# More output buffers, later sends and a cast on another engine in a fused GCN and mixture-of-experts kernel

## The chip, the cores and the metric

The kernel runs on one core of one Trainium2 chip. The metric is device time in microseconds of one execution, the median of several.

## What is computed

6250 nodes with 256 channels and 106,250 edges, then a layer with 16 experts of which each node uses two:

```python
def _L0_gnn_ref(x, edge_index, W1, b1, W2, b2):     # theta: GCN of the normalised x, averaged over nodes
    theta = _gcn_conv(x, edge_index, W1, b1)
    theta = jax.nn.relu(jnp.mean(theta, axis=0))
    theta = 2.0 * jax.nn.sigmoid(theta @ W2 + b2) - 1.0
    coefs = theta.reshape(C, 2 * k) * lambdas + init_v
    out = x[:, :, None] * coefs[None, :, :k] + coefs[None, :, k:]
    return jnp.max(out, axis=-1)

x = x + _L0_gnn_ref(_layernorm(x, axis=-1), edge_index, ...)
# feed-forward part, on layernorm(x):
topk_vals, topk_idx = jax.lax.top_k(x @ gate_w + gate_b, 2)
h = relu(x @ w1[e] + b1[e]); expert_out = h @ w2[e] + b2[e]      # for the two chosen experts
y = x + sum(softmax(topk_vals) * expert_out)
x = x + layernorm(y) * gamma + beta
```

Because theta is a mean over nodes, the aggregation needs only one weight per node: the degree of every node, its inverse root, and for each edge the value at the target added up at the source.

## The kernel before, in words

The code is written by hand for each engine: each has its own instruction list, in the order in which it runs, and semaphores tie them together. There are five stages.

**Degree stage.** Edges lie on 128 partitions in 832 columns, 26 groups of 32. For each group VectorE makes two one-hot arrays of the target (`onehot`, line 1288, called from the loop at line 1292), and TensorE multiplies them into the degree table (line 1020). Beside it ScalarE takes sums and squares of the 49 node tiles of x (lines 785 and 798). Behind the loop VectorE finishes the variance (line 1304) and ScalarE takes its root (line 817); the inverse root and the shift (lines 1323, 1324) follow, then the root of the degrees (line 819).

**Values stage.** For each group g of 32 edge columns VectorE selects keys (`select`, line 1315), makes two one-hots of the source (line 1288), casts the gathered values from PSUM (line 1351) and weighs the one-hot with them (line 1356, twice). TensorE runs in 104 slots, four to a group. Slot n is `rows_of(n)` (line 1040), `values_of(n - 1)` (line 1051) and `scatter(n - 8)` (line 1060). ScalarE masks each slot's rows (line 832) and puts the 49 normalising passes of x (line 842) between them. Group g's first rows need `select(g)`, and its weighted one-hots need the cast of its 64 value columns.

```python
dve.wait_ge(masked_free, 4 * g + 4)
nc.vector.tensor_copy(g16[:, u], PS[:, B_G + u, 0:2 * GC]...).then_inc(g_copied, 1)
```

**Routing stage.** Affine, maximum, second normalisation, gate, top two and slot numbers in eight groups of node tiles. GpSimd scatters each token row twice into its expert's place in `xs` (98 indirect DMAs, line 575). A tile of expert work needs that its rows have landed: the first ten tiles (`SOON`) need the first six groups, all others need all 98 scatters and 16 pad rows blocks (`pad_row`, one DMA of 128 rows per expert, issued by SyncE and ScalarE).

**Tile stage.** 113 tiles of 128 rows. TensorE runs `up(t)` (line 1224), `turn_x(t + 1)` (line 1212) and `down(t - 1)` (line 1235). VectorE runs in iteration t: `relu` (line 1562), `home_of(t + 1)` (lines 1572 and 1575), `share_of(t + 1)` (lines 1581 to 1585), `weigh_out(t - 1)` (line 1603) and `base_of(t)` (line 1594). GpSimd sends each finished tile from one of `OBUFS` buffers to `ys` by an indirect DMA with the row numbers in `home` (`send`, line 582). `down(t)` waits for `weigh_out(t - 1)`. The row numbers lie in 4 buffers, the outputs in 4; `home_of(t)` from tile 4 on waits until the send of tile t - 4 has landed:

```python
dve.wait_ge(o_sent[(t - XBUFS) % OBUFS], 16 * ((t - XBUFS) // OBUFS + 1))
```

GpSimd's list puts the first four sends between the last group's scatters. SyncE, in iteration t, issues the load of the weights of tile t + 4 and of the rows of tile t + 4; the iteration that loads tile 10 first waits for all scatters and all pads (lines 702 to 705).

**Last stage.** The two expert rows of each node are summed, normalised, scaled and stored, behind the landing of every send.

## Time and profile before

| | us |
|---|---|
| median of 3 runs (928.9 to 932.2) | 929.2 |
| the profiled execution's own time | 929.78 |
| its span, first to last instruction | 928.0 |
| TensorE busy | 770.7 (83%) |
| VectorE busy | 675.1 (73%) |
| ScalarE busy | 460.1 (50%) |
| GpSimd busy | 273.9 (30%) |
| mean granted TensorE clock | 0.911 |

An engine's busy time is summed over stages that have different limits, so the shares do not say what bounds a stage. The views below are read per stage; their times count from the start of the span. A wait is named after the instruction that came last. The granted clock is 1.0 at 2.4 GHz and 0.5 at 1.2 GHz, so a mean of 0.95 is a mix of the two.

### The profile page before, as it was taken

How to read it: one execution, taken by the hardware profiler on the slowest of the kernel's cores; microseconds unless marked ns; L12 is line 12 of the kernel's file. 1: busy time of each engine (PE TensorE's matmuls, PEld its weight loads, DVE VectorE, ACT ScalarE, POOL GpSimd, SP SyncE). 2: the span in 40 equal slices, each digit the busy share in tenths (PEclk: the TensorE clock that was granted, in tenths of full speed). 3: DMA queues.
4: the chain of work that ended last, by engine and by line, in shares of the span. 5: the costliest groups of instructions: out<-in, count | busy, mean ns of one | idle time of the engine just before them, and what ended most of it. 6: DMA issues, size and time to landing. Idle time of an engine off the chain costs nothing.

```text
span 928.0 us, 21948 instructions
## 1 busy us (share of the span) xinstructions
PE 770.7 (83%) x6539; PEld 673.4 (73%) x6539; DVE 675.1 (73%) x1856; ACT 460.1 (50%) x1161; POOL 273.9 (30%) x309
## 2 busy tenths in 40 slices
PE   3554988787866787676999999999999999997882
PEld 3454455555545786565899999999999999996771
DVE  6999899999927677854666666666666666664597
ACT  6980887787726657333333334433344333443253
POOL 9300000000001467777334444444322222222000
PEclk9999699999986667559899999999999999999896
DMA  9831444456155354269766666676766666662984
GB/s 275 233 116 35 129 162 144 143 163 196 59 182 171 100 171 137 104 228 288 207 215 215 214 211 212 210 214 215 213 213 207 211 216 213 212 211 64 380 313 135
DMA packets 88003, 174.88 MB, mean 188 GB/s; under 512 B 13067, under 2 KB 57022, under 8 KB 84796
## 3 DMA queue, kind: packets, MB, share of 16 engines
q1 hardware_dynamic: 74600, 143.83, 49.4%
q0 software_dynamic: 10512, 27.88, 8.5%
q10 hardware_dynamic: 2776, 1.77, 0.9%
q8 instruction: 56, 0.92, 0.4%
q14 instruction: 59, 0.48, 0.2%
HBM read 136.24 MB, written 37.20 MB: 187 GB/s over the span
## 4 chain that ended last, share of the span: by engine, by line
PE 54%; DVE 24%; issue 10%; POOL 7%; DMA 2%; ACT 2%; SPq 0%; DVEq 0%; POOLq 0%; ACTq 0%
PE PS L1224 21%; PE PS L1235 21%; DVE W L1288 10%; POOL xs L575 7%; DVE W L1315 3%; DVE W L1356 3%; PE PS L1212 3%; PE PS L1150 2%; PE PS L1265 2%; DVE W L1657 1%; DVE W L1664 1%; PE PS L1126 1%; DVE W L1634 1%; DMA ys<-W,R 1%; PE PS L1004 1%
## 5 line engine op out<-in xcount | busy, mean ns | idle before, releaser
L1224 PEld LDWEIGHTS PS<-R,W 128*128 128x128 f32 x1808 | 221.2, 193 | 7.6 <-ACT R L926 1.7
L1235 PE MATMUL PS<-W,R 128*128 x904 | 216.1, 382 | 9.9 <-DVE W L1603 8.3
L1224 PE MATMUL PS<-R,W 128*128 128x128 f32 x1808 | 222.0, 276 | 1.0 <-ACT R L926 1.0
L582 POOL DMA_INDIRECT ys<-W,R x113 | 109.8, 972 | 267.2 <-DVE W L1603 261.8
L1235 PEld LDWEIGHTS PS<-W,R 128*128 128x128 f32 x904 | 165.1, 193 | 28.9 <-issue 11.0
L926 ACT ACTIVATE R<-PS 128x256 f32<-128x256 f32 x113 | 43.6, 386 | 264.6 <-PE PS L1212 262.3
L1288 DVE TENSOR_TENSOR W<-R,W 128x3136 bf16<-128x3136 bf16 (+1 forms) x104 | 157.0, 1565 | 0.7 <-PE PS L1020 0.5
L1562 DVE TENSOR_SCALAR R<-PS,b1T 128x128 f32<-128x128 f32 x226 | 69.3, 349 | 113.8 <-PE PS L1224 109.5
L832 ACT ACTIVATE W<-PS 128x1024 f16<-128x1024 f32 x104 | 105.5, 1020 | 34.3 <-PE PS L1040 33.0
L575 POOL DMA_INDIRECT xs<-W,slot_i x98 | 98.0, 1000 | 80.0 <-DVE slot_i L1454 51.3
L1040 PE MATMUL PS<-W,table 114*128 114x512 f16 x208 | 68.4, 414 | 24.1 <-DVE W L1315 23.6
L943 ACT ACTIVATE R<-PS,b1T 128x128 f32<-128x128 f32 x226 | 70.4, 368 | 2.3 <-PE PS L1224 2.1
L1060 PE MATMUL PS<-W 128*98 128x128 bf16 x832 | 69.2, 228 | 2.7 <-DVE W L1356 2.7
L1020 PE MATMUL PS<-W 128*64 128x98 bf16 x832 | 42.7, 208 | 30.8 <-DVE W L1288 30.8
L567 POOL MEMSET R<- 128x261 f32 x1 | 0.3, 318 | 229.7 <-PEq L1082 229.7
L1051 PEld LDWEIGHTS PS<-sel,W 128*128 128x128 f16 x832 | 31.9, 98 | 46.2 <-ACT W L832 38.8
L1020 PEld LDWEIGHTS PS<-W 128*64 128x64 bf16 x832 | 39.3, 110 | 34.1 <-DVE W L1288 34.1
L952 ACT ACTIVATE W<-R 128x256 f32<-128x256 f32 x113 | 57.9, 513 | 4.3 <-DVE R L1572 4.3
L1060 PEld LDWEIGHTS PS<-W 128*98 128x98 f16 x832 | 56.3, 129 | 2.9 <-DVE W L1356 2.9
L1603 DVE SCALAR_TENSOR_TENSOR W<-PS,R,W 128x256 f32<-128x256 f32 x113 | 54.7, 484 | 5.0 <-PE PS L1235 4.8
L1265 PE MATMUL PS<-W,ident 128*128 128x256 f32 x196 | 47.2, 403 | 13.2 <-DMA W<-ys 8.0
L1265 PEld LDWEIGHTS PS<-W,ident 128*128 128x128 f32 x196 | 39.3, 203 | 21.1 <-DMA W<-ys 8.7
(249 smaller groups left out, 1117.0 us busy)
## 6 DMA issues: line engine op xcount, KB each, us to landing
W<-in_L_ffn_w SPq DMA_DIRECT2D x129, 512.0 KB, 3.7
W<-key_rows SPq DMA_DIRECT2D x26, 784.0 KB
R<-xs SPq DMA_DIRECT2D x113, 130.5 KB, 2.6
W<-ys SPq DMA_DIRECT2D x4, 2048.0 KB, 13.7
XH<-in_x SPq DMA_DIRECT2D x6, 896.0 KB, 11.8
out<-W SPq DMA_DIRECT2D x4, 1024.0 KB, 5.1
W<-in_x SPq DMA_DIRECT2D x4, 896.0 KB, 5.8
W<-key_rows SPq DMA_DIRECT2D x52, 64.0 KB
```

The costliest lines, as they stand in the source:

```text
L575: nc.gpsimd.indirect_dma_start(out=xs[:, :], out_offset=bass.IndirectOffsetOnAxis(ap=slot_i[0:rows, g % XNBUFS, j, k:k + 1], axis=0), in_= ...
L582: nc.gpsimd.indirect_dma_start(out=ys[:, :], out_offset=bass.IndirectOffsetOnAxis(ap=home[:, b:b + 1], axis=0), in_=O3[o], in_offset=None) ...
L832: act.activation(masked[0:2 * HD, n % 3, :].rearrange("p (h m) -> p h m", h=2), PS[0:2 * HD, bank:bank + 2, :], ACT.Relu).then_inc(masked_ ...
L943: last = act.activation(HT3[:, u, j, :], PS[:, 2 + 2 * u + j // 2, (j % 2) * P:(j % 2 + 1) * P], ACT.Relu, bias=b1T[:, ds(e, 1), j])
L1020: last = nc.tensor.matmul(PS[0:HD, B_DEG, 0:LOD], oh_hi[g % 2][:, c // 2, :, c % 2], oh_lo[g % 2][:, c // 2, 0:LOD, c % 2], start=(g == 0 ...
L1040: last = nc.tensor.matmul(PS[0:2 * HD, B_R + 2 * (n % 2) + h, :], table[0:KT, :], oh_t[0:KT, g % 2, at:at + 4 * P], start=True, stop=True)
L1060: last = nc.tensor.matmul(PS[0:2 * NT, B_ACC, 0:P], weighted[g % 2][:, c // 2, :, c % 2], oh_lo[g % 2][:, c // 2, :, c % 2], start=(n == 0 ...
L1224: last = nc.tensor.matmul(PS[:, 2 + 2 * u + j // 2, (j % 2) * P:(j % 2 + 1) * P], W1S[b][:, k, j * P:(j + 1) * P], XT3[:, u, k, :], start= ...
L1235: last = nc.tensor.matmul(PS[:, 6, 0:C], HT3[:, u, j, :], wt2(e * W2COLS, j), start=(j == 0), stop=(j == 3))
L1265: last = nc.tensor.matmul(y_sum(g, j), ident[:, :], y_two[g % YBUFS][:, j, k, :], start=(k == 0), stop=(k == 1))
L1288: return nc.vector.tensor_tensor(into, pairs_of.to_broadcast([P, GC // 2, size, 2]), iota2[:, 0:size, :].unsqueeze(1).to_broadcast([P, GC ...
L1562: last = nc.vector.tensor_scalar(HT3[:, u, j, :], PS[:, 2 + 2 * u + j // 2, (j % 2) * P:(j % 2 + 1) * P], b1T[:, ds(e, 1), j], 0.0, ALU.ad ...
```

## The change

It has five parts.

1. `OBUFS` goes from 4 to 8, and `home` gets a ring of its own of `HBUFS` = 12. `home_of(t)` waits for a send only from tile 12 on, `weigh_out(t)` from tile 8 on. The buffers Z1 and Z3 of the tile stage move to the space of gW2 to make room.
2. GpSimd issues all 98 scatters first and every send after them.
3. The 16 pads are spread over six tiles: SyncE issues two ahead of the loop and one in each of six iterations, ScalarE two in each of iterations 0 and 1 and one in each of 2 to 5. The loads of gamma and beta go from iteration 4 to 6.
4. The variance, inverse root and shift are computed inside VectorE's degree loop (behind groups 20 and 21), and ScalarE does 28 of the 49 normalising passes there, ahead of the root of the degrees. The other 21 follow one to a group, behind slots 4k + 3.
5. The cast of the values goes from VectorE to ScalarE. The cast of group g stands behind the masking of slot 4g + 5.

```diff
@@ -65,7 +65,7 @@
 W2COLS = C * F // P
 W1BUFS = 4
 XW = C + 5
-XBUFS, OBUFS = 4, 4
+XBUFS, OBUFS, HBUFS = 4, 8, 12
 SOON, SOON_G = 10, 5
 XNBUFS = 3
 X_AT = E * WCOLS * 4 - 2 * GT * C * 4
@@ -210,12 +210,10 @@
         share = take([XBUFS], fp32)
         first = take([XBUFS], fp32)
         weight = take([XBUFS], fp32)
-        home = take([XBUFS], i32)
+        home = take([HBUFS], i32)
         assert at[0] <= RB
         take, at = carve(W, D_AT + 4 * XNBUFS * GT * XW)
         O3 = [take([C], fp32) for _ in range(OBUFS - 1)] + [O_last]
-        Z1 = take([2, C], fp32)
-        Z3 = take([2, C], fp32)
         assert at[0] <= D_AT + 4 * (XNBUFS * GT * XW + GT * 2 * P)
 
         take, at = carve(W, E * W2COLS * 4)
@@ -244,7 +242,12 @@
         gw_sb = sb("gw_sb", [P, 2, E], fp32)
         gateb_bc = sb("gateb_bc", [P, E], fp32)
         gb1_col = sb("gb1_col", [HID, 1], fp32)
-        gW2_sb = sb("gW2_sb", [HID, 4 * C], fp32)
+        gW2_all = sb("gW2_all", [P, 4 * C], fp32)
+        gW2_sb = gW2_all[0:HID, :]
+        take, at = carve(gW2_all, 0)
+        Z1 = take([2, C], fp32)
+        Z3 = take([2, C], fp32)
+        assert at[0] <= 4 * C * 4
         gb2_col = sb("gb2_col", [P, 2, 4], fp32)
         zcol = sb("zcol", [P, 2, 4], fp32)
         coef = sb("coef", [P, 2, 4], fp32)
@@ -577,10 +576,10 @@
                             in_=xn[0:rows, g % XNBUFS, j, :], in_offset=None).then_inc(xn_sent[g % XNBUFS], 16)
 
                 def send(t):
-                    b, o = t % XBUFS, t % OBUFS
+                    h, o = t % HBUFS, t % OBUFS
                     pool.wait_ge(o_ready, t + 1)
                     nc.gpsimd.indirect_dma_start(
-                        out=ys[:, :], out_offset=bass.IndirectOffsetOnAxis(ap=home[:, b:b + 1], axis=0),
+                        out=ys[:, :], out_offset=bass.IndirectOffsetOnAxis(ap=home[:, h:h + 1], axis=0),
                         in_=O3[o], in_offset=None).then_inc(o_sent[o], 16)
 
                 for g in range(NDG - 1):
@@ -588,12 +587,8 @@
                     for j in range(DG[g][1]):
                         scatter(g, j)
                 pool.wait_ge(slots_ready, NDG)
-                sent = 0
                 for j in range(DG[NDG - 1][1]):
                     scatter(NDG - 1, j)
-                    if j >= 2:
-                        send(sent)
-                        sent += 1
 
                 def add_beta(t):
                     if t == 0:
@@ -601,7 +596,7 @@
                     nc.gpsimd.tensor_tensor(XH[:, t, :], XH[:, t, :], beta_bc, ALU.add).then_inc(beta_added, 1)
                     pool.wait_ge(beta_added, t + 1)
 
-                for t in range(sent, MT):
+                for t in range(MT):
                     if 12 <= t < 12 + NT:
                         add_beta(t - 12)
                     send(t)
@@ -687,7 +682,7 @@
                 for t in range(XBUFS):
                     load(t)
                 sp.wait_ge(pads_ready, 1)
-                for e in range(4):
+                for e in range(2):
                     pad_row(sp, e)
                 for t in range(MT):
                     if t + W1BUFS < MT:
@@ -704,8 +699,8 @@
                                 sp.wait_ge(xn_sent[b], sends(max(g for g in range(NDG) if g % XNBUFS == b)))
                             sp.wait_ge(pads_in, 16 * (E + 1))
                         load(t + XBUFS)
-                    if t < 4:
-                        pad_row(sp, 4 + t)
+                    if t < 6:
+                        pad_row(sp, 2 + t)
                 sp.wait_ge(mm2_done, MT)
                 for b in range(OBUFS):
                     sp.wait_ge(o_sent[b], 16 * ((MT - 1 - b) // OBUFS + 1))
@@ -815,6 +810,15 @@
 
                 act.wait_ge(var_ready, 1)
                 act.activation(sd[:, :], lnsq[:, :], ACT.Sqrt).then_inc(sd_ready, 1)
+                act.wait_ge(norm_ready, 1)
+
+                def normalise_x(t):
+                    act.activation(XH[:, t, :], XH[:, t, :], ACT.Identity, bias=nmr[:, t:t + 1],
+                                   scale=rstd[:, t:t + 1]).then_inc(xhat_ready, 1)
+
+                EARLY_X = 28
+                for t in range(EARLY_X):
+                    normalise_x(t)
                 act.wait_ge(deg_ready, 1)
                 act.activation(rootA[0:LOD, :], degA[0:LOD, :], ACT.Sqrt).then_inc(deg_rooted, 1)
 
@@ -822,8 +826,15 @@
                 act.activation(disT[0:HD, :], PS[0:HD, B_DIS, 0:LOD], ACT.Copy).then_inc(dis_copied, 1)
                 act.wait_ge(dis_copied, 1)
                 act.dma_start(dis_lin.rearrange("(h l) -> h l", l=LOD), disT[0:HD, :]).then_inc(dis_stored, 16)
-                act.wait_ge(norm_ready, 1)
-                normalised = 0
+                def cast(g):
+                    u = g % 2
+                    act.wait_ge(masked_free, 4 * g + 4)
+                    if g >= 2:
+                        act.wait_ge(weighted_ready, g - 1)
+                    act.activation(g16[:, u], PS[:, B_G + u, 0:2 * GC].rearrange("p (c k) -> p k c", k=2), ACT.Copy
+                                   ).then_inc(g_copied, 1)
+
+                normalised = EARLY_X
                 for n in range(NSLOT):
                     act.wait_ge(rows_out, n + 1)
                     if n >= 3:
@@ -837,11 +848,12 @@
                     if n == NSLOT - 8:
                         act.wait_ge(dis_back, 1)
                         act.activation(dis[:, :], PS[:, B_DIS, LOD:LOD + NT], ACT.Copy).then_inc(dis_copied, 1)
-                    while normalised < NT and normalised * (NSLOT - 8) < (n - 3) * NT:
-                        t = normalised
-                        act.activation(XH[:, t, :], XH[:, t, :], ACT.Identity, bias=nmr[:, t:t + 1],
-                                       scale=rstd[:, t:t + 1]).then_inc(xhat_ready, 1)
+                    if n >= 5 and n % 4 == 1:
+                        cast(n // 4 - 1)
+                    elif normalised < NT and n % 4 == 3:
+                        normalise_x(normalised)
                         normalised += 1
+                cast(NG - 1)
                 assert normalised == NT
 
                 act.activation(warm[:, 0:1], ones1[:, :], ACT.Sigmoid).then_inc(warmed, 1)
@@ -963,12 +975,13 @@
                     if t + 1 < MT:
                         ratio_of(t + 1)
                     keep(t)
-                    if t < 4:
+                    if t < 6:
                         act.wait_ge(pads_ready, 1)
                         act.wait_ge(zrows_set, 3)
-                        pad_row(act, 8 + 2 * t)
-                        pad_row(act, 9 + 2 * t)
-                    if t == 4:
+                        pad_row(act, 8 + t)
+                        if t < 2:
+                            pad_row(act, 14 + t)
+                    if t == 6:
                         act.dma_start(gamma_bc, gamma.partition_broadcast(P)).then_inc(rows_in, 16)
                         act.dma_start(beta_bc, beta.partition_broadcast(P)).then_inc(rows_in, 16)
 
@@ -1292,16 +1305,20 @@
                 for g in range(NG):
                     if g >= 2:
                         dve.wait_ge(deg_free, g - 1)
-                    onehot(oh_lo[g % 2][:, :, 0:LOD, :], dlo, g, LOD).then_inc(deg_lo, 1)
+                    onehot(oh_lo[g % 2][:, :, 0:LOD, :], dlo, g, LOD)
                     onehot(oh_hi[g % 2], dhi, g, HD).then_inc(deg_onehots, 1)
                     if g == 3:
                         dve.wait_ge(src_in, 32)
                         dve.wait_ge(dst_split, 4)
                         nc.vector.tensor_scalar(tmp_i, src_i, P - 1, None, ALU.bitwise_and).then_inc(src_ints, 1)
                         nc.vector.tensor_scalar(hi_i, src_i, LO_BITS, None, ALU.logical_shift_right).then_inc(src_ints, 1)
-
-                dve.wait_ge(sq_done, 1)
-                nc.vector.tensor_scalar(lnsq[:, :], lnsq[:, :], 1.0 / C, EPS, ALU.mult, ALU.add).then_inc(var_ready, 1)
+                    if g == 20:
+                        dve.wait_ge(sq_done, 1)
+                        nc.vector.tensor_scalar(lnsq[:, :], lnsq[:, :], 1.0 / C, EPS, ALU.mult, ALU.add).then_inc(var_ready, 1)
+                    if g == 21:
+                        dve.wait_ge(sd_ready, 1)
+                        link(nc.vector.reciprocal(rstd[:, :], sd[:, :]))
+                        nc.vector.tensor_tensor(nmr[:, :], nmean[:, :], rstd[:, :], ALU.mult).then_inc(norm_ready, 1)
 
                 dve.wait_ge(deg_free, NG)
                 nc.vector.tensor_scalar(degT[0:HD, :], PS[0:HD, B_DEG, 0:LOD], 1.0, None, ALU.add).then_inc(deg_copied, 1)
@@ -1319,9 +1336,6 @@
                 dve.wait_ge(deg_turned, 1)
                 nc.vector.tensor_copy(degA[0:LOD, :], PS[0:LOD, B_G, 0:HD]).then_inc(deg_ready, 1)
 
-                dve.wait_ge(sd_ready, 1)
-                link(nc.vector.reciprocal(rstd[:, :], sd[:, :]))
-                nc.vector.tensor_tensor(nmr[:, :], nmean[:, :], rstd[:, :], ALU.mult).then_inc(norm_ready, 1)
                 dve.wait_ge(src_split, 2)
                 onehot(oh_hi[0][:, :, 0:NT, :], shi, 0, NT).then_inc(src_hot, 1)
                 dve.wait_ge(deg_rooted, 1)
@@ -1346,10 +1360,7 @@
                         onehot(oh_hi[u][:, :, 0:NT, :], shi, g, NT).then_inc(src_hot, 1)
                     if g >= 2:
                         dve.wait_ge(scattered, g - 1)
-                    onehot(oh_lo[u], slo, g, P).then_inc(src_lo, 1)
-                    dve.wait_ge(masked_free, 4 * g + 4)
-                    nc.vector.tensor_copy(g16[:, u], PS[:, B_G + u, 0:2 * GC].rearrange("p (c k) -> p k c", k=2)
-                                          ).then_inc(g_copied, 1)
+                    onehot(oh_lo[u], slo, g, P)
                     dve.wait_ge(g_copied, g + 1)
                     dve.wait_ge(src_hot, g + 1)
                     for k, done in ((0, weighted_half), (1, weighted_ready)):
@@ -1564,15 +1575,16 @@
                     last.then_inc(relu_dve, 1)
 
                 def home_of(t):
-                    b = t % XBUFS
+                    b, h = t % XBUFS, t % HBUFS
                     dve.wait_ge(x3_in[b], 16 * (t // XBUFS + 1))
                     if t >= XBUFS:
                         dve.wait_ge(kept_ready, t - XBUFS + 1)
-                        dve.wait_ge(o_sent[(t - XBUFS) % OBUFS], 16 * ((t - XBUFS) // OBUFS + 1))
+                    if t >= HBUFS:
+                        dve.wait_ge(o_sent[(t - HBUFS) % OBUFS], 16 * ((t - HBUFS) // OBUFS + 1))
                     nc.vector.tensor_scalar(first[:, b:b + 1], X3[:, b, C + 2:C + 3], et_bc[:, t:t + 1], None, ALU.is_equal
                                             ).then_inc(first_ready, 1)
                     dve.wait_ge(first_ready, t + 1)
-                    nc.vector.tensor_scalar(home[:, b:b + 1], X3[:, b, C + 4:C + 5], first[:, b:b + 1], trash[:, t:t + 1],
+                    nc.vector.tensor_scalar(home[:, h:h + 1], X3[:, b, C + 4:C + 5], first[:, b:b + 1], trash[:, t:t + 1],
                                             ALU.subtract, ALU.min).then_inc(home_ready, 1)
 
                 def share_of(t):
```

On VectorE, one group of the values stage. Line 1315 (line 1332 after) is `select`, the two that follow are the one-hots, the last two the weighted one-hots. Before:

```order
L1315 TENSOR_SCALAR W<-W,keyp 114x4096 [waits rows_out,key_in1]
L1288 TENSOR_TENSOR W<-R,W 128x16x98 [waits weighted_ready]
L1288 TENSOR_TENSOR W<-R,W 128x4096 [waits scattered]
L1351 CAST R<-PS 128x64 [waits masked_free]
L1356 TENSOR_TENSOR W<-W,R 128x16x98 [waits src_hot,g_copied]
L1356 TENSOR_TENSOR W<-W,R 128x16x98
```

And now:

```order
L1332 TENSOR_SCALAR W<-W,keyp 114x4096 [waits rows_out,key_in1]
L1301 TENSOR_TENSOR W<-R,W 128x16x98 [waits weighted_ready]
L1301 TENSOR_TENSOR W<-R,W 128x4096 [waits scattered]
L1367 TENSOR_TENSOR W<-W,R 128x16x98 [waits src_hot,g_copied]
L1367 TENSOR_TENSOR W<-W,R 128x16x98
```

The cast has left VectorE, and `g_copied` is now signalled by ScalarE.

On ScalarE, now, from the root of the variance (line 812) to the second group of values; line 816 is a normalising pass, line 823 the root of the degrees, line 843 the masking of a slot, line 834 the cast:

```order
L812 ACTIVATE sd<-R 128x49 [waits var_ready]
L816 ACTIVATE XH<-XH,nmr,rstd 128x256 [waits norm_ready]
L816 ACTIVATE XH<-XH,nmr,rstd 128x256 x27
L823 ACTIVATE W<-W 98x64 [waits deg_ready]
L826 ACTIVATE W<-PS 64x98 [waits dis_turned]
L828 DMA dis_lin<-W 64x98 [waits dis_copied]
L843 ACTIVATE W<-PS 128x1024 [waits rows_out] x3
L843 ACTIVATE W<-PS 128x1024 [waits masked_free,rows_out]
L816 ACTIVATE XH<-XH,nmr,rstd 128x256
L843 ACTIVATE W<-PS 128x1024 [waits masked_free,rows_out] x2
L834 ACTIVATE R<-PS 128x64 [waits masked_free]
L843 ACTIVATE W<-PS 128x1024 [waits masked_free,rows_out] x2
```

Twenty-eight passes stand ahead of the root of the degrees, and the first group's cast stands behind the masking of slot 5.

On GpSimd, the end of the scatters (line 575, line 574 after) and the first sends (line 582, line 581 after). Before:

```order
L575 DMA xs<-W,slot_i 102528x261 x5
L582 DMA ys<-W,R 27008x256 [waits o_ready]
L575 DMA xs<-W,slot_i 102528x261 x2
L582 DMA ys<-W,R 27008x256 [waits o_ready]
L575 DMA xs<-W,slot_i 102528x261 x2
L582 DMA ys<-W,R 27008x256 [waits o_ready]
L575 DMA xs<-W,slot_i 102528x261 x2
L582 DMA ys<-W,R 27008x256 [waits o_ready] x9
```

And now:

```order
L574 DMA xs<-W,slot_i 102528x261 x13
L574 DMA xs<-W,slot_i 102528x261 [waits slots_ready]
L574 DMA xs<-W,slot_i 102528x261 x11
L581 DMA ys<-W,R 27008x256 [waits o_ready] x12
L596 TENSOR_TENSOR XH<-XH,W 128x256 [waits rows_in]
```

Six scatters that stood behind the first send now stand ahead of it.

## Rows read from the trace of the kernel before

**Rows 1.** Busy times by stretch: us; PE, PEld, DVE, ACT, POOL busy; PEclk, DMA, GB/s.

```profile
101.00:251.00 150.00, 123.78 (x1716) 82.73 (x1716) 148.99 (x142) 117.91 (x146) 0.00 (x0) 0.95 0.47 147
...
432.00:442.00 10.00, 3.09 (x25) 2.67 (x23) 2.20 (x9) 1.59 (x5) 5.76 (x6) 0.84 1.04 336
442.00:855.00 413.00, 410.49 (x2822) 386.59 (x2822) 264.70 (x981) 161.13 (x540) 146.92 (x162) 1.00 0.65 205
```

**Rows 2.** The chain that ended last, around tile 3: start us, us, what.

```profile
432.03 8.14 DMA ys<-W,R
...
441.31 0.48 DVE W L1603
...
445.77 1.78 PE PS L1224 x16
...
447.79 1.73 PE PS L1235 x8
```

**Rows 3.** Timeline of TensorE and VectorE, 432 to 442 us: start, us, what, idle before.

```profile
434.69 0.40 PE L1212 MATMUL PS<-ident,R 128*128 128x128 f32 x2
442.03 3.35 PE L1235 MATMUL PS<-W,R 128*128 x7 [6.95 <-DVE W L1603]
...
432.46 0.61 DVE L1562 TENSOR_SCALAR R<-PS,b1T 128x128 f32<-128x128 f32 x2 [0.59 <-issue]
440.31 0.21 DVE L1572 TENSOR_SCALAR R<-R,et_bc 128x1 f32<-128x1 f32 x1 [7.24 <-DMA ys<-W,R]
```

**Rows 4.** GpSimd's timeline at the last scatters, and their landings.

```profile
432.03 0.96 POOL L582 DMA_INDIRECT ys<-W,R  x1 [0.30 <-issue]
...
445.20 1.56 POOL L575 DMA_INDIRECT xs<-W,slot_i  x1 [0.30 <-issue]
...
DMA to landing us min/median/max: 5.0/7.0/8.6
```

**Rows 5.** DMA issues from 380 to 445 us: median us to landing.

```profile
R<-xs SPq DMA_DIRECT2D x9, 130.5 KB, 4.8
```

**Rows 6.** Timeline of one group of the values stage on four engines.

```profile
164.72 1.28 DVE L1315 TENSOR_SCALAR W<-W,keyp 114x4096 f16<-114x4096 f16 x1
165.92 3.17 DVE L1288 TENSOR_TENSOR W<-R,W 128x1568 bf16<-128x1568 bf16 x2
166.06 0.60 PE L1040 MATMUL PS<-W,table 114*128 114x512 f16 x2 [1.21 <-DVE W L1315]
...
166.70 2.14 ACT L832 ACTIVATE W<-PS 128x1024 f16<-128x1024 f32 x2 [1.27 <-PE PS L1040]
...
168.74 0.59 ACT L842 ACTIVATE XH<-XH,nmr,rstd 128x256 f32<-128x256 f32 x1
...
169.00 0.22 DVE L1351 CAST R<-PS 128x64 f16<-128x64 f32 x1
...
169.26 1.86 DVE L1356 TENSOR_TENSOR W<-W,R 128x1568 f16<-128x1568 bf16 x2
...
171.03 1.28 DVE L1315 TENSOR_SCALAR W<-W,keyp 114x4096 f16<-114x4096 f16 x1
```

**Rows 7.** Timeline of the first groups of the values stage.

```profile
99.05 1.02 ACT L832 ACTIVATE W<-PS 128x1024 f16<-128x1024 f32 x1 [0.28 <-PE PS L1040]
...
99.24 0.23 DVE L1351 CAST R<-PS 128x64 f16<-128x64 f32 x1 [2.72 <-PE PS L1051]
...
105.10 1.05 PE L1040 MATMUL PS<-W,table 114*128 114x512 f16 x2
```

**Rows 8.** Timelines around the end of the degree stage, and of later passes.

```profile
71.89 1.63 PE L1020 MATMUL PS<-W 128*64 128x98 bf16 x32 [1.21 <-DVE W L1288]
...
85.95 0.17 DVE L1304 TENSOR_SCALAR R<-R 128x49 f32<-128x49 f32 x1
...
86.16 0.24 ACT L817 ACTIVATE sd<-R 128x49 f32<-128x49 f32 x1 [20.99 <-DVE R L1304]
...
394.95 2.06 ACT L891 ACTIVATE W<-XH,nmr,rstd 128x256 f32<-128x256 f32 x4
```

6 lines of the change are left out of this document (1 added, 5 removed).

## The prediction

> **What bounds the kernel now.** I read the busy times by stretch first, then the chain of waits, then the timelines of the places that the change touches. The tile stage is TensorE's: from 442 to 855 us it is busy 410.5 of 413 us at a granted clock of 1.00 [rows 1], one tile each 3.75 us (up to down 2.02 us, down to the next up 1.73 us) [rows 2]. Nothing in the change makes that period shorter. The values stage is VectorE's: busy 149.0 of 150 us [rows 1], one group each 6.31 us (164.72 to 171.03) [rows 6]. The degree stage too: TensorE waits 1.21 us a group for the one-hots, while ScalarE idles 21.0 us until VectorE's line 1304 [rows 8]. Between routing and the steady tile stage lies a hole: TensorE is busy 3.1 of the 10 us from 432 [rows 1]. The chain says why. The first send is issued at 432.03 behind the scatters and takes 8.14 us to land; `home_of(4)` waits for it until 440.31, `weigh_out(2)` behind it starts at 441.31, and down(3) behind that at 442.03 [rows 2, 3]. So two places can pay: that hole, and VectorE's 6.31 us.
>
> **The hole (parts 1 and 2).** VectorE's relu of tile 3 ends at 432.46 + 0.61 = 433.07 [rows 3]. Without the wait, home, share and `weigh_out(2)` follow at once; from `home_of` to `weigh_out` it was 441.31 - 440.31 = 1.0 us, and the result takes 0.48 us [rows 2, 3], so it is there at 434.6. TensorE ends its transposes for tile 5 at 434.69 + 0.40 = 435.1 [rows 3], and is now the later one. Down(3) therefore starts at 435.1 in place of 442.03. It ran on the half-rate clock behind the hole (3.35 us for seven matmuls [rows 3], and up(5) came 3.74 us after it); with no hole it takes the steady 1.73 us. Up(5) starts at 436.8, not 445.77 [rows 2]: **9.0 us less**. From there VectorE has an iteration of about its old length and TensorE the longer one, so tiles follow at 3.75 us.
>
> What is late next? Three things.
> - The sends. Six scatters stood behind the first send; a scatter takes 0.96 + 0.30 us on GpSimd [rows 4], so the last is issued at 432.03 + 5 x 1.26 = 438.3 in place of 445.20, and send(0) at about 439.6. `weigh_out(8)` is the first to wait for it, near 436.8 + 3 x 3.75 + 7 = 455; landing takes 8.14 us at the worst seen. No wait. GpSimd is behind by five sends, and catches up 2.5 us on each tile.
> - The rows of tile 10. Their load waits for all scatters and all pads. Scatters land 5.0 to 8.6 us after issue [rows 4]: 443.3 to 446.9. The last pads are now issued in iteration 5, at about 442.4 by my count of SyncE's and ScalarE's iterations; a pad's landing is not in the trace, and I bound it by nothing beyond its issue below (443) and the slowest scatter above (451.0). The load itself takes 4.8 us in this crowded stretch [rows 5]. TensorE wants the rows behind up(9), at 436.8 + 4 x 3.75 + 1.8 = 453.6. With a median scatter's 7.0 us: 449.4 + 0.5 + 4.8 = 454.7, one over; with the rows' own 4.8 us for a pad of the same 130 KB in its place, 452.5, one under. I take 0 and keep 0 to 2.7 us for the range. All rings are full here, 1.04 busy at 336 GB/s [rows 1].
> - The weights of tile t + 4 are asked for four tiles ahead, 15 us; nothing else moves in SyncE's queue but two pads less ahead of it.
>
> **The pads (part 3)** are 16 as before. VectorE, not ScalarE, is last in tiles 0 to 3, so ScalarE's two issues fewer in tiles 2 and 3 gain nothing, and one each in 4 and 5 hides under the 3.75 us. 0 us.
>
> **The degree stage (part 4).** Line 1304 (0.17 us, 0.2 with its wait) ran in the shadow of the last matmuls [rows 8] and now stands in VectorE's bound loop: **+0.2 us**. Lines 1323 and 1324 were on the path and still are. A group takes 1.63 + 1.21 = 2.84 us [rows 8]; group 21 ends near 74.8 (four groups ahead of 85.95, plus 0.2), the shift is there at 75.4. Four passes of ScalarE take 2.06 us [rows 8], a pitch of 0.49 us, so 28 end at 75.4 + 13.8 = 89.2. The root of the degrees is wanted at about 90.0 and used at 90.9, behind a one-hot. Nothing is late. If each pass took its full 0.59 us [rows 6] instead, they would end at 91.9 and cost 1.3 us: the bound.
>
> **The cast (part 5).** On VectorE the cast costs 169.26 - 169.00 = 0.26 us of each group [rows 6]. Without it the weighting could start at 169.00. It now waits for ScalarE: select ends, TensorE's rows start at 166.06, ScalarE masks two slots from 166.70 and is free at 168.74 [rows 6]; a cast of about 0.25 us (line 817 has 49 columns in 0.24 us [rows 8]) and a hop of about 0.05 us give 169.04. So 0.22 us is kept, and the two ways are level: VectorE has no slack left against ScalarE. Groups 3 to 24: 22 x 0.22 = **4.8 us**, and 0.25 us in the last, where there is no select.
> The start pays for it. The cast of group 0 ran at 99.24 and now stands behind the masking of slots 4 and 5; slot 4's began at 99.05 [rows 7]. Two of 1.0 us and the cast: weighting starts at 101.3 in place of 99.50, **1.8 us late**. Group 1 meets the half-rate clock: two pairs of rows at 1.05 us in place of 0.60 [rows 6, 7], and narrow matmuls between, make the detour about 1.2 us longer (estimate), 0.9 net. Group 2 gets back about 0.5. Start: 2.2 us lost. And 0.95 over 150 us [rows 1] is 15 us at half rate; 6 are group 1, the other 9 make 1.4 groups x 1.2 = 1.6 us lost. Part 5 is worth 4.8 + 0.25 - 2.2 - 1.6 = **1.2 us**; its ends are +3.1 (no half-rate loss, 1.8 at the start) and -2 (three more half-rate groups).
>
> The rule against this part stands in the Trainium skill, ScalarE: Activation LUTs, Rules for kernel authors: adds, maxima and the like belong on VectorE, which is faster per element. By the figures in its section What ACT_TABLE_LOAD costs, 64 columns with immediates take 186 + 0.833 x 64 = 239 ns (estimate from that page) against the trace's 0.22 us on VectorE. Judged by the operation alone the move loses 26 x 0.02 = 0.5 us. The rows say that the queue matters and not the operation: ScalarE idles 1.27 us in the group, VectorE never.
>
> **Sum.** 9.0 - 0.2 + 1.2 = 10.0 us. The profiled execution took 929.8 us, 0.6 more than the median: 919.8 there, **919.2** as a median. About 0.5% (4.6 us) is what a measurement here can tell from no change.
>
> **The rivals.**
> 1. The wait for landed sends is replaced by one for landed pads and scatters: the load of tile 10 comes late. For: rings full, pads issued later than before. Against: TensorE still has ten tiles of which it needs none of this. Price 1 to 5 us: 920 to 924; 921.9 with a pad as slow as the slowest scatter. 14%.
> 2. The detour is longer than VectorE's work: ScalarE's cast comes 0.2 us after the one-hot in every group (a hop of 0.25 us). Then 4.8 us are gone: 924.0. For: level by my count. Against: TensorE's and ScalarE's waits in the rows show short hops. With half of that, 921.6. 12%.
> 3. No change. The rings at 1.04 are the true limit from 420 us on, and the work moved ahead only makes TensorE wait at tile 10 instead of at tile 3. Then the 9.0 us are gone: 928.2. Against: from 442 us on the rings are 0.65 busy [rows 1], so the queue is not long. 6%.
> 4. Slower. TensorE, waiting for the later selects of the first groups, is less busy, and the clock stays at half rate. A half-rate group costs at least 6.31 + 0.94 = 7.25 us against 6.09. Gain and loss meet at about 9 such groups beyond the 2.4 counted; at 17 it is 919.2 + 17 x 1.16 = 939. Against: at half rate TensorE's own work fills the group, and in the rows it returned to full rate under the same load. 3%. The Trainium skill, TensorE: Matmul & The Clock Gate, Part 1, has the half rate as the default which sustained activity releases; by that rule the gaps added at the start would make this likelier, and in the trace the pairs of rows do run at 1.05 us at first and at 0.60 later.
>
> **How the numbers follow.** My forecast has 65%. Its own range: 12.5 us gained (no loss to the half rate, 1.8 at the start) to 7.5 us, 916.7 to 921.7. The range for 8 in 10 takes in most of rivals 1 and 2: **915.8 to 923.3**. Faster by over 0.5%, under 924.6: forecast, rivals 1 and 2 and a little less, 0.90. Within: 0.07. Slower: 0.03.
>
> **What would show it.** Right: no wait for a send in iterations 3 to 11; down(3) right behind the transposes of tile 5; up(5) 9 us sooner, counted from the first up; the last scatter before send(0); a period of 6.07 to 6.12 us in the values stage; root of the degrees not later than its input. Wrong: VectorE idle in each group ahead of the weighting for ScalarE's cast; TensorE idle ahead of tile 10's transposes; a granted clock well under 0.95 from 101 to 245 us; 28 passes that end after VectorE's degree copy.

## The result and the profile after

| | before | after |
|---|---|---|
| median of four runs, us | 930.3 | 919.8 (918.2 to 921.2) |
| profiled execution, us | 929.8 | 921.2 |
| its span, us | 928.0 | 919.4 |
| granted clock over the span | 0.911 | 0.905 |

The ratio is 0.9885, 95% interval 0.9856 to 0.9915; a second batch on another chip gave 0.9886. The forecast was 919.2 us, in a range of 915.8 to 923.3. The kernel before has one more run here than in the table ahead of the prediction, which moves its median from 929.2 to 930.3. The sum came out; several of its terms did not, and they missed in opposite directions, so that part of the hit is luck.

The busy times of the changed kernel by stretch, with the columns of [rows 1]; the first, third and fourth answer to the three rows there:

```profile
101.00:251.00 150.00, 124.48 (x1758) 82.18 (x1757) 147.37 (x123) 113.73 (x146) 0.00 (x0) 0.97 0.47 147
280.00:411.00 131.00, 95.98 (x517) 87.98 (x515) 92.78 (x423) 74.22 (x148) 76.51 (x78) 0.62 0.47 155
425.00:434.00 9.00, 7.95 (x55) 7.08 (x54) 6.13 (x27) 3.44 (x12) 6.82 (x7) 1.00 1.04 316
434.00:845.00 411.00, 408.71 (x2822) 385.52 (x2821) 264.69 (x980) 161.71 (x544) 148.19 (x164) 1.00 0.66 211
```

TensorE is busy 7.95 of 9 us where it was 3.09 of 10; the period of the tiles behind is 3.75 us as before. Its timeline there, and GpSimd's below it:

```profile
433.08 0.40 PE L1225 MATMUL PS<-ident,R 128*128 128x128 f32 x2
433.72 1.99 PE L1248 MATMUL PS<-W,R 128*128 x8 [0.24 <-DVE W L1615]
435.54 1.95 PE L1237 MATMUL PS<-R,W 128*128 128x128 f32 x16
...
436.08 1.55 POOL L574 DMA_INDIRECT xs<-W,slot_i  x1 [0.30 <-issue]
437.94 0.98 POOL L581 DMA_INDIRECT ys<-W,R  x1 [0.30 <-issue]
```

Down(3) waits 0.24 us where it waited 6.95 [rows 3], and up(5) starts at 435.54, not 445.77 [rows 2]. Send(0) is issued behind the last scatter, at 437.94, and nobody waits for it. One group of the values stage, as in [rows 6]:

```profile
165.84 1.28 DVE L1332 TENSOR_SCALAR W<-W,keyp 114x4096 f16<-114x4096 f16 x1
...
167.03 3.17 DVE L1301 TENSOR_TENSOR W<-R,W 128x1568 bf16<-128x1568 bf16 x2
...
167.82 2.14 ACT L843 ACTIVATE W<-PS 128x1024 f16<-128x1024 f32 x2 [1.02 <-PE PS L1053]
...
169.86 0.22 ACT L834 ACTIVATE R<-PS 128x64 f16<-128x64 f32 x1
...
170.12 1.85 DVE L1367 TENSOR_TENSOR W<-W,R 128x1568 f16<-128x1568 bf16 x2
...
171.89 1.28 DVE L1332 TENSOR_SCALAR W<-W,keyp 114x4096 f16<-114x4096 f16 x1
```

165.84 to 171.89 is 6.05 us a group, against 6.31. The cast ends at 170.08. The one-hots end at 167.03 + 3.17 = 170.20, and what follows them starts some 0.08 before such an end (before, 169.00 for 169.09 [rows 6]). So both let the weighting start at 170.12: level, as counted. And the start:

```profile
101.99 0.22 ACT L834 ACTIVATE R<-PS 128x64 f16<-128x64 f32 x1
...
102.24 1.86 DVE L1367 TENSOR_TENSOR W<-W,R 128x1568 f16<-128x1568 bf16 x2 [4.70 <-ACT R L834]
...
105.36 1.03 PE L1053 MATMUL PS<-W,table 114*128 114x512 f16 x2 [1.43 <-DVE W L1332]
...
109.57 1.86 DVE L1367 TENSOR_TENSOR W<-W,R 128x1568 f16<-128x1568 bf16 x2 [1.19 <-ACT R L834]
```

The cast was at 99.24 [rows 7], the first weighting at 99.50 and the second at 105.81; now the weightings stand at 102.24 and 109.57, and VectorE waits 4.70 and 1.19 us for ScalarE's cast.

### The profile page after: what moved, and what is told of

Its sections match the earlier page's. It is cut to its first block, busy times and chain, and to the rows that moved or that the text cites. A ratio compares the mean times of both kernels' runs of the same rounds, so it can differ in the third digit from the quotient of the medians.

```text
span 919.4 us, 21975 instructions
## 1 busy us (share of the span) xinstructions
PE 775.1 (84%) x6539; PEld 676.0 (74%) x6539; DVE 668.9 (73%) x1830; ACT 467.1 (51%) x1187; POOL 272.6 (30%) x309
## 4 chain that ended last, share of the span: by engine, by line
PE 63%; DVE 25%; issue 7%; ACT 2%; DMA 1%; DVEq 0%; POOL 0%; SPq 0%; ACTq 0%; POOLq 0%
PE PS L1237 21%; PE PS L1248 21%; DVE W L1301 7%; PE PS L1163 4%; DVE W L1332 3%; DVE W L1367 3%; PE PS L1053 3%; PE PS L1225 3%; PE PS L1139 2%; PE PS L1278 2%; PE PS L1017 2%; PE PS L1073 1%; DVE W L1669 1%; DVE W L1676 1%; PE PS L1151 1%
## 5 line engine op out<-in xcount | busy, mean ns | idle before, releaser
L574 POOL DMA_INDIRECT xs<-W,slot_i x98 | 97.1, 990 | 81.3 <-DVE slot_i L1465 52.7
L1033 PE MATMUL PS<-W 128*64 128x98 bf16 x832 | 47.7, 220 | 27.2 <-DVE W L1301 27.2
L1033 PEld LDWEIGHTS PS<-W 128*64 128x64 bf16 x832 | 44.1, 119 | 30.7 <-DVE W L1301 30.7
L964 ACT ACTIVATE gW_all<-R 128x256 f32<-128x256 f32 x113 | 57.8, 512 | 0.0
L1615 DVE SCALAR_TENSOR_TENSOR W<-PS,R,gW_all 128x256 f32<-128x256 f32 x113 | 54.8, 485 | 3.6 <-PE PS L1248 3.3
## 6 DMA issues: line engine op xcount, KB each, us to landing
R<-xs SPq DMA_DIRECT2D x113, 130.5 KB, 2.5
```

Of the source, the lines that this page charges most:

```text
L574: nc.gpsimd.indirect_dma_start(out=xs[:, :], out_offset=bass.IndirectOffsetOnAxis(ap=slot_i[0:rows, g % XNBUFS, j, k:k + 1], axis=0), in_= ...
L1033: last = nc.tensor.matmul(PS[0:HD, B_DEG, 0:LOD], oh_hi[g % 2][:, c // 2, :, c % 2], oh_lo[g % 2][:, c // 2, 0:LOD, c % 2], start=(g == 0 ...
```

## The experiments

Twelve runs of ten kernels in three batches, each batch on one chip and beside the kernel before. On the chip of the first batch the kernel before took 973.0 us, on the other two 931.7 and 931.4, so those say most. The ratios are those of the comparison that gave the interval, not quotients of the medians; where two kernels are compared below, the two ways can differ by 2 us, and then both are given. This table cuts the trace of each kernel of these two batches at the same points (the first two rows are the traces shown above): the copy of the accumulated table by VectorE, the start of up(0), of up(5) and of the last up, and the end. 107 tiles of 3.75 us are 401.25 us; "over" is what up(5) to the last up takes beyond that.

| kernel | median (its batch's before) | table copied | to up(0) | up(0) to up(5) | over | rest |
|---|---|---|---|---|---|---|
| before | 930.3 | 261.8 | 151.8 | 32.0 | 0.0 | 81.1 |
| after | 919.8 (930.3) | 258.5 | 154.5 | 22.6 | 0.7 | 81.9 |
| after, second batch | 922.5 (931.7) | 258.7 | 153.5 | 22.9 | 3.1 | 81.2 |
| parts 1 to 3 | 925.5 (931.7) | 261.9 | 151.8 | 23.2 | 2.9 | 81.1 |
| part 2 alone | 939.1 (931.7) | 261.5 | 155.1 | 37.7 | 0.6 | 81.3 |
| part 1 alone | 928.6 (931.4) | 261.7 | 155.2 | 23.1 | 4.4 | 81.7 |
| after, pads over four tiles | 924.3 (931.4) | 257.7 | 153.0 | 22.8 | 6.3 | 81.0 |
| after, early cast | 917.6 (931.7) | 257.2 | 148.1 | 23.0 | 4.7 | 81.7 |
| the same, fewer bytes of W1 | 914.6 (931.4) | 255.4 | 152.8 | 22.2 | 0.7 | 82.4 |
| the same, five buffers of rows | 917.0 (931.4) | 254.8 | 152.2 | 22.8 | 2.4 | 81.4 |

**The change itself again.**

> The changed kernel itself, beside the other runs of this batch. In all runs so far of the edits apart, the routing stage of both kernels was some 43 us longer than in the trace of before (972.98 us for before), and GpSimd had finished its scatters before the third tile, so that there was no hole to close. My theory (hole 9.0 to 9.6 us, values stage 0.26 us per group, start 1 to 2 us lost): where before takes about 929 us, the whole change gives 0.9885 of it as first measured, 919 us; where before takes about 973 us and has no hole, only the values stage's part is left, 0.994 to 1.000 of before. Rival (the gain is not the hole but lies in the values stage): the ratio is 0.989 in either case.

922.5 us, 0.9886 (0.9857 to 0.9916). Up(5) comes 22.9 us after up(0), so the hole is closed; but this execution loses 3.1 us right behind it, which the first trace of after (0.7) hardly showed. TensorE's timeline says where:

```profile
437.65 0.50 PE L1225 MATMUL PS<-ident,R 128*128 128x128 f32 x2 [0.56 <-DMA R<-xs]
438.61 1.99 PE L1248 MATMUL PS<-W,R 128*128 x8 [0.46 <-issue]
```

These are the transposes of tile 6: they wait for its rows. SyncE's timeline has that load at 427.56, 10 us earlier.

**The hole alone.** The edit is parts 1 to 3 on the kernel before; the degree and values stages stay. First on the chip where before takes 973 us:

> Parts 1 to 3 alone (buffers, sends behind the scatters, pads over six tiles); degree and values stage as before. Theory (the hole is worth 9.0 us, independent of the rest): no wait for a send in tiles 4 to 11, up(5) 22.9 us behind up(0) in place of 32.2; 9.3 us (8.5 to 10) less than before, so about 920.5. Rival (parts 4 and 5 bring more than my 1.0 us and the hole less): 923 or more. Rival (the whole gain is this, the rest is worth nothing): equal to the changed kernel within 1 us.

974.6 us, 1.0019 (1.0008 to 1.0030): nothing gained. Its chain and GpSimd's timeline tell why:

```profile
445.38 26.40 another core or an unknown queue
```

```profile
467.42 1.56 POOL L574 DMA_INDIRECT xs<-W,slot_i  x1 [0.30 <-issue]
478.96 0.98 POOL L581 DMA_INDIRECT ys<-W,R  x1 [9.98 <-DVE W L1599]
```

ScalarE stands still for 26.4 us behind the first tile, for a reason that the trace doesn't name. GpSimd does not: it has ended its scatters at 469 and then waits 9.98 us for the first output. Where the tiles start that late there is no send that stands behind scatters, and no hole. The kernel of parts 4 and 5 alone (below), which has the sends of before, bears this out in the same batch: its `home_of(4)` waits for no landed send, and the later ones up to 500 us 0.3 us in all, where before waited 7.24. All four kernels of that batch had these stalls: from the table's copy to up(0) they took 181 to 185 us in place of 148 to 155, and up(0) to up(5) took 40 to 45. Their values stages ran as elsewhere. The kernel before is 43 us slower there by the medians. Then on a chip like the first:

> Parts 1 to 3 alone once more (eight buffers, twelve columns of home rows, sends behind the scatters, pads over six tiles), with the degree and values stages of before. My theory: where before takes about 929 us, its trace has the 9.9 us hole before up(5) and this kernel has none: 9 us faster than before, 920 us (ratio 0.990), so that it makes nearly all of the change's gain; where before takes about 973 us, the same time as before within 0.3%, as the first run of it had. Rival (the values stage makes the gain): within 0.2% of before in either case.

925.5 us, 0.9942 (0.9921 to 0.9963): 6.2 us by the medians, 5.4 by the ratio, where 9 were expected. Again the timeline of TensorE:

```profile
435.12 1.89 PE L1231 MATMUL PS<-W,R 128*128 x8
436.85 1.95 PE L1220 MATMUL PS<-R,W 128*128 128x128 f32 x16
...
451.92 1.99 PE L1231 MATMUL PS<-W,R 128*128 x8 [0.36 <-issue]
```

Down(3) at 435.12 and up(5) at 436.85 are the forecast's 435.1 and 436.8. The table has the rest: 8.8 us less from up(0) to up(5), then 2.9 given back in four pieces of 0.5 to 1.0 us, ahead of up(6), up(7), up(9) and up(10). The rows put them down to "issue" or, once, to VectorE's relu, and none to a load.

**The order alone (part 2).**

```
                 for j in range(DG[NDG - 1][1]):
                     scatter(NDG - 1, j)
-                    if j >= 2:
-                        send(sent)
-                        sent += 1
...
```

> Before with one edit, part 2 alone: the sends of the last tiles behind all scatters, in the old four buffers and four columns of home rows. My theory: buffers and order belong together. send(0) is issued some 5 us later (about 439.6 instead of 434.4 in the time of the trace of before), home_of(4) waits for its landing that much longer, and the hole before up(5) grows from 9.9 to some 15 us: 5 to 8 us slower than before where before takes about 929 us (ratio 1.005 to 1.009); the same time as before where the scatters end before the tiles run (973 us). Rival (the order alone closes the hole, because down(3) no longer stands behind a GpSimd that alternates): faster by several us.

939.1 us, 1.0084 (1.0061 to 1.0107): 7.4 us slower, as my theory has it. The spans of the two traces are 9.5 apart: 5.7 between up(0) and up(5), and 3.3 in a routing stage that differs between executions. VectorE and TensorE in its trace:

```profile
449.05 0.21 DVE L1568 TENSOR_SCALAR R<-R,et_bc 128x1 f32<-128x1 f32 x1 [12.93 <-DMA ys<-W,R]
```

```profile
450.78 3.78 PE L1231 MATMUL PS<-W,R 128*128 x8 [12.77 <-DVE W L1599]
```

`home_of(4)` waits 12.93 us for send(0) in place of 7.24 [rows 3], and down(3) 12.77 in place of 6.95. With four buffers the later sends make the hole deeper.

**The buffers alone (part 1).** `OBUFS` 8, `HBUFS` 12, the sends between the scatters as before, the pads over four tiles.

> Before with part 1 alone: eight output buffers and twelve columns of home rows, but the sends still alternate with the last scatters and the pads go over four tiles. My theory: home_of(4) no longer waits for a landing, so the hole before up(5) closes here too; but the three or four sends between the scatters put off the last scatter by some 1.3 us each, 4 to 5 us in all, so that tile 10 can be loaded that much later. Tile 10 had 0 to 1 us to spare in the traces with the sends behind, so 3 to 5 us of waiting for R<-xs appear at turn_x(10): 2 to 5 us faster than before (ratio 0.995 to 0.998). Rival (the last scatter's landing has slack): as fast as parts 1 to 3 together, ratio 0.994.

928.6 us, 0.9971 (0.9955 to 0.9988), inside what was expected, and not for the reason given. The hole is closed (23.1 us), but 4.4 us come back, and not at tile 10:

```profile
443.76 0.50 PE L1211 MATMUL PS<-ident,R 128*128 128x128 f32 x2 [1.79 <-DMA R<-xs]
```

This is tile 6. Of tile 10, whose load really was issued later (455.40), TensorE waits for nothing. So the buffers close the hole by themselves. What the order adds to them is not shown: this kernel differs from parts 1 to 3 in the pads as well, and with the pads over four tiles the traces give back 4.4 us without the later sends and 6.3 with them (next run).

**The pads (part 3).** The change with its pads over four tiles again.

> The changed kernel with the pads over four tiles again, as before (part 3 undone). In the traces of the change the DMA rings are full from the third to the seventh tile, and turn_x of tiles 6 and 7 waits 0.6 to 1.9 us for loads that took 7 to 12 us. Theory A (the loads are late because of all that is queued in the rings): 16 pads of 130.5 KB in the first four tiles make the loads of tiles 4 to 7 later still, 0.5 to 2 us slower than the whole change (ratio to before 0.989 to 0.991). Theory B, as I predicted blind: 0 within 0.3 us, since the same bytes pass.

924.3 us, 0.9934 (0.9911 to 0.9956). Against before that is 7.1 us by the medians, and the change has 9.3 to 10.5: 2 to 3 us lost, or 4.5 by the ratios, where 0.5 to 2 were expected. The two intervals just overlap, so the size is loose. The place is not. TensorE, and SyncE's issue of the same load:

```profile
439.63 0.70 PE L1224 MATMUL PS<-ident,R 128*128 128x128 f32 x2 [4.21 <-DMA R<-xs]
440.49 3.20 PE L1247 MATMUL PS<-W,R 128*128 x8 [0.16 <-issue]
```

```profile
426.79 0.34 SPq L671 DMA_DIRECT2D R<-xs  x1
```

The rows of tile 6 take 12.8 us to come, TensorE waits 4.21, and goes on at half rate for a tile (3.20 us in place of 1.89). Theory A holds; the prediction's 0 us does not.

**Do the rings make the loads late?** The rings are the queues of the core's DMA engines; I call them full where the DMA share is about 1.0. Two edits on the kernel with the early cast (below). In the first, the loads of W1 for tiles 4 to 9 bring one row each:

```
+                        if t + W1BUFS < SOON:
+                            u = (t + W1BUFS) % W1BUFS
+                            sp.dma_start(W1S[u][0:1]..., w1[0:1, 0:2, :]...).then_inc(w1_in[u], 16)
+                        else:
+                            load_w1(t + W1BUFS)
```

It leaves out 3 MB of weights; tiles 4 to 9 compute with what the buffers hold.

> The kernel with the early cast (r_early_again: 0.9856 of before), in which the loads of W1 for tiles 4 to 9 bring one row of each instead of 512 KB, 3 MB less in the stretch where the DMA share is 1.0 (tiles 4 to 9 then use what lies in the buffers). It tells whether the rings make the late loads. Theory A (full rings): R<-xs land some 5 us after their issue instead of 8.0, turn_x waits for no load, up(0) to the last up takes 423.5 to 424.5 us instead of 429.0, and the kernel is 3 to 5 us faster than r_early_again, ratio 0.981. Rival (SP's own order of issues makes the loads late, not the bytes): the same waits and 0.9856.

914.6 us, 0.9821 (0.9791 to 0.9851), against 0.9856 (0.9830 to 0.9882) for its base: 2.6 us more gained by the medians and 3.3 by the ratios, where 3 to 5 were expected. The intervals overlap, so the times alone don't settle it. The rows of the DMA view, 405 to 450 us, first of the base, then of this kernel (issues, KB each, median us to landing):

```profile
W<-in_L_ffn_w SPq DMA_DIRECT2D x8, 512.0 KB, 9.7
...
R<-xs SPq DMA_DIRECT2D x8, 130.5 KB, 8.0
```

```profile
R<-xs SPq DMA_DIRECT2D x10, 130.5 KB, 4.0
```

The rows land in 4.0 us and not in 8.0, no wait of TensorE is put down to a load, and 0.7 us are given back in place of 4.7; up(0) to the last up takes 424.2 us, as expected. That 0.7 by itself proves little, since the first trace of the change has it too. The landings do more, if they are counted at the same place in each kernel: over the loads issued from 4 to 30 us behind up(0), those of tiles 4 to 9, their median is 7.6, 8.5, 10.3 and 10.3 us in the first trace of the change, in parts 1 to 3, in the second trace of the change and in the base, at a DMA share of 0.99 to 1.02. In this kernel:

```profile
R<-xs SPq DMA_DIRECT2D x6, 130.5 KB, 3.6
```

with a DMA share of 0.72. So the bytes in the rings make the loads late, not SyncE's order. The 0.7 us now stands at another tile: behind the transposes of tile 10, at 447.18, whose load was issued only at 443.79, behind the scatters and pads. Its row says "issue"; that tile 10 is the next limit is likely, not shown. The second edit gives the loads more time: `XBUFS` 5, so that the rows of tiles 5 to 9 are asked for one tile earlier.

> The kernel with the early cast and five buffers for the rows of a tile instead of four, so that the loads of tiles 5 to 9 are issued one tile (some 4.4 us) earlier; SP issues load_w1(10) ahead of the load of tile 10, and the pads go over five tiles. Theory: loads that took 8 to 12 us are covered, turn_x(7) and turn_x(8) wait no more for R<-xs, 2 to 4 us faster than r_early_again (ratio 0.982 to 0.984), with the remainder of the delay at tile 10, which still waits for the last scatters. Rival: the bytes only come earlier into rings that are already full, so that W1 or tile 10 come late instead: the same 0.9856.

917.0 us, 0.9862 (0.9833 to 0.9892), the same as its base: the rival. Its DMA view:

```profile
W<-in_L_ffn_w SPq DMA_DIRECT2D x8, 512.0 KB, 10.9
R<-xs SPq DMA_DIRECT2D x9, 130.5 KB, 8.7
```

No transposes wait for rows any more, but rows and weights take longer still, and 2.4 us are given back in small pieces, one behind a wait of 0.70 us ahead of up(7). That this one is late weights is an inference; the row says only "issue".

**The values stage.** The degree and values stages of the change on the kernel before (parts 4 and 5):

> Parts 4 and 5 alone (28 passes and the shift in the degree stage, cast on ScalarE); tile stage as before with 4 buffers, interleaved sends and the old pads. Theory: 0.2 us lost in the degree loop, 1.7 lost at the first group of values, 0.9 at the second, 0.26 gained in each group after it: the values stage from table to last weighting 3.5 us shorter, 1 to 3 us less in all by what the half-rate clock takes. Rival (nothing reaches the end, since routing eats it): within 0.5 us of before. The hole of 7 us in front of home_of(4) is there as before.

And the change with the cast back on VectorE:

> The changed kernel with the cast put back on VectorE, everything else kept. Theory (the cast on ScalarE is what moves the values stage): a group takes 6.31 us again in place of 6.05, the first weighting starts 1.7 us sooner and the second 2.7 sooner; 3.5 us slower at the last weighting, 2 to 4 us slower than the changed kernel as a whole. Rival (the period fell because passes left ScalarE, not because of the cast): the period stays 6.05 and the kernel is 2 us faster.

Both ran in the first batch (before 973.0 us): 967.9 us, 0.9960 (0.9947 to 0.9973), and 974.8 us, 1.0028 (1.0017 to 1.0039). Their traces separate the two parts. With part 4 but the cast on VectorE the first weighting starts at 99.68, against 99.59 in the kernel of parts 1 to 3 there; the table is copied at 261.80, against 261.73. So part 4 costs 0.1 us and buys nothing by itself. With the cast on ScalarE the weightings start at 100.82 and 108.16 (99.68 and 106.00 without), and the table is copied at 256.76: 5.0 us sooner. With the cast back on VectorE a group takes 6.31 us again, though the passes have left ScalarE's list there too, so it is the cast that makes the period. Of the 5.0 us only 3.6 stand at the last weighting (252.77 for 256.38). The other 1.4 come behind it, in TensorE's last 32 multiplications into the table, first with the cast on VectorE, then on ScalarE:

```profile
258.30 3.46 PE L1070 MATMUL PS<-W 128*98 128x128 bf16 x32 [2.74 <-DVE W L1367]
```

```profile
254.68 2.05 PE L1076 MATMUL PS<-W 128*98 128x128 bf16 x32 [2.22 <-DVE W L1370]
```

That is the half rate and the full one. From the last weighting to the copy the six traces with the cast on VectorE have 5.3 to 5.4 us, the eight with it on ScalarE 4.0 to 5.5, so this piece differs from one execution to the next. Two things in what was expected of parts 4 and 5 alone did not come: they gained 5.1 us by the medians, not 1 to 3, and the wait of 7 us at `home_of(4)` was not there.

**The early cast.** One line of the change:

```
-                    if n >= 5 and n % 4 == 1:
+                    if n >= 4 and n % 4 == 0:
```

> The changed kernel with the cast of group g behind the masking of slot 4g + 4, one slot sooner. Theory (the first two groups wait for ScalarE's later cast; in the steady groups VectorE is the limit by now): first weighting 1.0 us sooner, second 2.0 sooner, period 6.05 unchanged; 1 to 2.5 us faster than the changed kernel. Rival (VectorE's steady period is still set by ScalarE's cast): the period falls below 6.0 and the gain is 3 us or more.

> The changed kernel with ScalarE's cast of group g behind the masking of slot 4g+4 instead of 4g+5, so that a group's weighting waits for one masking less. If the wait for the cast at the start (weighting(0) and group 1, together some 2.7 us late in the trace of after) is due to the two maskings ahead of the cast, this kernel is 1.5 to 3 us faster than the whole change on the same chip (ratio 0.997 to 0.998 of it); in the steady groups the cast comes a masking earlier and nothing changes, 6.05 us per group. Rival: the start is bound by TensorE at half rate, then under 0.5 us.

In the first batch 967.5 us, 0.9960 (0.9945 to 0.9975), where the whole change was not run. In the second 917.6 us, 0.9856 (0.9830 to 0.9882), 4.9 us below the change by the medians and 2.8 by the ratios; the intervals overlap, and the traces give the part that is shown. ScalarE, then VectorE:

```profile
100.85 0.22 ACT L834 ACTIVATE R<-PS 128x64 f16<-128x64 f32 x1
```

```profile
101.10 1.86 DVE L1367 TENSOR_TENSOR W<-W,R 128x1568 f16<-128x1568 bf16 x2 [3.73 <-ACT R L834]
...
107.16 1.86 DVE L1367 TENSOR_TENSOR W<-W,R 128x1568 f16<-128x1568 bf16 x2
```

The second weighting stands at 107.16 with no wait, in the change beside it at 109.41: 2.25 us, inside the 1.5 to 3 expected. At the table's copy 1.5 of them are left (257.2 for 258.7); in the first batch, beside parts 4 and 5 alone, 2.2 (254.5 for 256.8). The steady group stays at 6.05 or 6.06 us though the cast comes a slot sooner, so in the steady groups VectorE's own work sets it and not ScalarE's detour, which answers rival 2. The remaining 2.6 us of the medians I can't place: this execution's routing was 5.5 us shorter, and its loads late by 4.7. This is the fastest kernel of the study that computes everything, together with the one of five buffers.

## Why the prediction was right, and where it was not

**The hole, 9.0 us: right where it was aimed, and partly given back.** Up(0) to up(5) took 32.0 us before and 22.6, 22.9 and 23.2 in three traces with parts 1 to 3: 9.4, 9.1 and 8.8 us. No VectorE instruction of the tile stage waits for a landed send in the change. It is the buffers that close the hole (23.1 us with them alone); the order alone makes it deeper. The step that failed is the look at what is late next. "Rows of tile 10" was the wrong tile: its load is held back by scatters and pads, in after by 2.8 and 2.2 us, but it lands in time. Late are tiles 6 to 8, whose loads wait for no scatter and no pad and yet take 10 to 13 us in full rings; I had taken the 4.8 us of [rows 5], a median over the 65 us from 380, and the rings are full only in the last 24 of them. Over the loads issued from 4 to 30 us behind up(0) the same trace of before has this:

```profile
R<-xs SPq DMA_DIRECT2D x5, 130.5 KB, 7.5
```

Through that, 0.7 to 3.1 us came back in the change; in the trace with 3.1 a named wait for rows stands at the head of it, in the one with 0.7 none does. Rival 3 (the rings as the true limit) was refused because they are 0.65 busy from 442 us on; that is why it doesn't take all, but over some six tiles it takes up to a third.

**The pads, 0 us: wrong.** Undone, they cost 2 to 3 us by the medians and 4.5 by the ratios, with 6.3 us over in the trace. They were costed at ScalarE's and SyncE's issues, which are hidden; what counts is that by the end of tile 3 four pads of 130.5 KB more have been put into the rings.

**The degree stage, 0.2 us: right in the clean pair.** With the cast on VectorE, 0.1. In the change the copy of the degrees came 1.6 us later (90.75 for 89.11), and the end of the stage 1.0 (93.95 for 92.93). Of this 0.7 is the three small operations inside the loop (steps of 2.93 and 3.45 us in place of 2.84), which the later chain gets back, and the rest goes with a half-rate clock early in the stage (a granted clock of 0.62 from 26 to 34 us in the second batch's trace of the change, 1.00 before). It was below 1.00 there in five of the nine traces with part 4 and in none of the five without; the edits touch nothing before group 20 but a semaphore, and whether they bring it is not shown. The 28 passes ended at 90.2 and the root was not late.

**The cast, 1.2 us: too small, 3 to 5 measured.** The steady step was right: 0.26 us a group (6.05 for 6.31) where 0.22 was counted. So was the sign of the start. Its size in the clean comparison was 1.1 us at the first weighting and 2.2 at the second, where 1.8 and 2.7 stood in the working; in the change itself 2.7 and 3.8, with the 1.0 us of the degree stage in it. The step that failed is "the other 9 us make 1.4 groups, 1.6 us lost". In the change no group after the second was longer for the clock but one, of 6.34 us; all others took 6.05 or 6.06, and the last, which has no `select`, 4.86. The clock in the row of 101 to 251 us is 0.97 where I had charged for 0.95, and a lower one does not cost a group by itself: with the cast back on VectorE it was 0.92, and the last weighting came at 256.38, against 256.41 in parts 1 to 3 of that batch with 0.96. Up to the last weighting the change gained 2.4 us (253.97 for 256.42); the 0.8 us more at the table's copy lie in the multiplications behind it, which no term of the sum had. The rule that adds, maxima and the like belong on VectorE (the Trainium skill, ScalarE: Activation LUTs, Rules for kernel authors) does not name a cast; held against this one, it is answered by the rows: the cast takes 0.22 us on either engine, and the kernel with it back on VectorE loses 5.0 us by the time the table is copied.

**Not foreseen: the routing.** From the table's copy to up(0), in instructions that all these kernels share, before took 151.8 us and the change 154.5 and 153.5. The other traces don't make this the change's doing: 151.8 and 155.1 to 155.2 without the cast on ScalarE, 148.1 to 154.5 with it. So the forecast's 10.0 us was 9.0 - 0.2 + 1.2, and the two traces shown have 9.4 (hole) - 0.7 (late loads) + 3.3 (to the table's copy) - 2.7 (routing) - 0.8 (last stage) = 8.5, for the 8.6 us between their spans; the medians are 10.5 apart. The sum was better than its terms, and that is luck: the cast's surplus about paid for the routing.

The ends that the prediction gives its own forecast do not follow from its terms either: 9.0 - 0.2 + 3.1 is 11.9 us gained and 9.0 - 0.2 - 2 is 6.8, where it has 12.5 and 7.5.

## What to carry to other kernels

When a stall is removed, price the next one by the worst landing in the stretch that now gets denser, not by the median over a wider window; and look at each transfer that is asked for there, also those that wait for nothing. Bytes that can be had earlier or later than a stretch with full rings are worth moving even if every issue is hidden. An operation is worth moving to an engine that is no faster at it if its own has no idle time and the other has; what it then costs lies at the start, where its new place in the queue is behind work that the old one wasn't behind.
